# Attention sums normalised on GpSimd instead of on TensorE and VectorE, in a two-layer convolution kernel

## The chip, the cores and the metric

One core of one Trainium2 chip runs the kernel. The metric is the device time of one execution in microseconds (us). Engines by their names in the profile: PE is TensorE's matrix multiplication and PEld its weight load, DVE is VectorE, ACT is ScalarE, POOL is GpSimd, and SP (SPq) is the engine that issues the DMAs.

## The reference

The input is 16 images of 64 channels and 128 x 128 pixels, f32. Layer 0 adds a median term to every channel, upsamples by two with a 7-tap filter, applies a ReLU and downsamples again. Layer 1 gates the image in the frequency domain and runs an attention in which every pixel is a query and 320 positions (256 of a stride-8 and 64 of a stride-16 convolution) are keys, with 4 heads of 16 channels:

```python
attn = jax.nn.softmax(jnp.einsum('bhqd,bhkd->bhqk', q, k) * scale, axis=-1)
out = jnp.einsum('bhqk,bhkd->bhqd', attn, v)
out = out.transpose(0, 2, 1, 3).reshape(b, n, c)
out = out @ proj_w + proj_b
return out.transpose(0, 2, 1).reshape(b, c, h, w) + x
```

The change is in the last step of the softmax, the division of the weighted values by the sum of the weights, and in the projection behind it.

## The kernel before

The kernel loops over the 16 images. Each round has a convolution part, a spectrum part, the keys and values, and at its end the attention loop, which this change touches. Every engine has its own program (`tensor`, `vector`, `scalar`, `gpsimd`, `sync`) with the order of its work written out by hand; semaphores join them, and an engine that waits holds up all that is behind it in its own program.

The attention loop has NT = 32 tiles t of 512 queries. A tile has ten steps w. In step w TensorE computes one group of scores into PSUM bank 0 or 1 (`scores`, L735 for w below 8, L740 for 8 and 9) and ScalarE takes the exp (L1185); scores w wait for the exp of scores w - 2, because they share a bank. Beside this, in steps 0 to 7 of tile t, TensorE computes the maxima's matmuls of tile t + 2 (`maxima`, L714), which VectorE reduces (L978); at step 8 VectorE splits the reduced maxima in two bf16 parts (`split_max`, a cast at L986 and a subtraction at L988), TensorE transposes them at step 1 of the next tile (`lay_max`, L722), ScalarE copies them (L1168), and SP lays them into the queries by DMA (L1336).

The weighted values of tile t - 1 are summed on TensorE at steps 2, 4 and 7 of tile t (`weigh`, L760) into bank 7: 128 partitions of values and sums of weights by 512 queries. What follows is the part that the change replaces:

- ScalarE copies bank 7 to OR at step 8 (L1180).
- TensorE transposes it to queries by channels at step 9 (`denominators`, four transposes, L770).
- VectorE takes the reciprocal of the sums (L1010) and multiplies (L1014) at step 0 of the next tile.
- TensorE transposes back at step 4 (`turn_back`, two transposes, L778); ScalarE copies to OX (L1192).
- TensorE multiplies by the projection at step 6 (`project_out`, L785); VectorE adds the result to the image in SBUF (Z) at step 7 (L1024).

The loops run over t up to NT + 1 for that, so two tiles' rest comes behind the last scores, with a few filler matmuls (`busy`).

Some tiles carry more. `stage` computes the queries of later tiles at the steps named in STAGES: in tiles 0, 1, 4 to 7 and 12 to 15, a matmul on TensorE (L649, in bank 7 behind the reader of the sums), an activation on ScalarE (L1145), a subtraction on VectorE (L931), a cast and a subtraction on GpSimd (L1268, L1270). SP loads the next units of queries (`load_unit`, six DMAs a tile, L394), in tiles 24 to 27 the next image (`load_image`, two DMAs a tile), and at tile 28 half of the one after (`load_next`). GpSimd adds the median to the next image (`add_median`, L384, two additions of 128x1024 in each of the tiles 28 to 31 of its program, which runs ahead of the others as soon as the loads have landed). In the depthwise convolution of the values, ahead of the loop, GpSimd multiplies (L1283) and adds (L1287).

## Time and profile before

| | |
|---|---|
| median of 3 runs | 11580.47 us (11576.59 to 11598.01) |
| profiled execution, its own time | 11584.36 us |
| its span | 11582.8 us |
| busy: TensorE, VectorE, ScalarE, GpSimd | 90%, 76%, 63%, 24% |
| granted TensorE clock, mean | 0.978 |

All rows are from that one execution. Its span runs from the first to the last instruction; the own time is 1.6 us longer. The last image's attention loop lies at the span's end, so its times are near 11250 to 11570. "x" is a count; a row of a timeline gives the start, the length and what was done; an arrow with an engine behind it names what ended a wait.

### The profile page before, as it was taken

To read this page: it belongs to the slowest core of one execution; us is meant where nothing else is said; L and a number is where in the kernel's file an instruction comes from. 1 tells how busy PE (TensorE), PEld (TensorE's weight loads), DVE (VectorE), ACT (ScalarE), POOL (GpSimd) and SP (SyncE) were. 2 spreads that over 40 slices of the span, in tenths; PEclk is the share of its full clock that TensorE was granted. 3 is DMA by queue.
4 is the path that set the end of the run, shared out by engine and by line. 5 is a ranking of instruction groups with operands and counts; after the bars stand their busy time and mean duration, and the time that the engine had idled before them with its cause. 6 is when DMAs were issued, how large, how long until landed. Compare 5 with 4: busy or idle time off the path is not lost. (4 is left out here: it accounts for less than half of the span.)

```text
span 11582.8 us, 198561 instructions
## 1 busy us (share of the span) xinstructions
PE 10455.8 (90%) x71885; PEld 5275.3 (46%) x72029; DVE 8796.4 (76%) x15082; ACT 7250.1 (63%) x12109; POOL 2763.8 (24%) x5217
## 2 busy tenths in 40 slices
PE   2898998989989899899989989899898998989999
PEld 1544445344454544535445354444534445354453
DVE  7877777777777777778777787777777777777776
ACT  5667565675656757567575666756567565675756
POOL 2313213122131221312223131221312213122130
PEclk9999999999999999999999999999999999999999
DMA  2021221212213022130211302122121221202213
GB/s 65 20 47 46 47 64 29 49 35 51 60 31 59 31 48 56 35 61 34 42 51 42 69 20 47 46 47 64 30 52 32 52 59 32 57 31 50 54 37 74
DMA packets 176857, 537.70 MB, mean 46 GB/s; under 512 B 64904, under 2 KB 87560, under 8 KB 154448
## 3 DMA queue, kind: packets, MB, share of 16 engines
q1 hardware_dynamic: 175952, 525.31, 20.1%
q8 instruction: 608, 9.96, 0.4%
q14 instruction: 297, 2.43, 0.1%
HBM read 232.49 MB, written 71.30 MB: 26 GB/s over the span
## 5 line engine op out<-in xcount | busy, mean ns | idle before, releaser
L978 DVE TENSOR_REDUCE R<-ps 128x2 f32<-128x640 f32 x4096 | 3185.4, 818 | 906.3 <-PE ps L714 904.8
L1185 ACT ACTIVATE R<-ps 128x512 f32<-128x512 f32 x5120 | 2821.4, 594 | 654.5 <-PE ps L735 628.9
L258 ACT ACTIVATE R<-R,st 128x1475 bf16<-128x1475 f32 (+1 forms) x1326 | 2077.1, 1566 | 489.6 <-DVE st L330 464.9
L319 DVE TENSOR_SCALAR_CACHE_REDUCE R<-R,st 128x1255 bf16<-128x1255 f32 (+1 forms) x1326 | 1936.8, 1461 | 18.5
L714 PE MATMUL ps<-KST,R 96*128 96x320 bf16 x8192 | 1811.8, 302 | 38.8 <-DVE R L978 29.5
L760 PE MATMUL ps<-R 128*32 128x512 f32 x12288 | 1641.0, 607 | 37.9 <-DVE Wk L931 32.8
L735 PE MATMUL ps<-R,KST 104*128 104x512 bf16 x4096 | 1569.6, 386 | 36.9 <-ACT R L1185 23.7
L714 PEld LDWEIGHTS ps<-KST,R 96*128 96x128 bf16 x8192 | 757.6, 99 | 736.6 <-DVE R L978 223.8
L1268 POOL CAST R<-Wk 128x512 bf16<-128x512 f32 x256 | 283.8, 1109 | 2492.7 <-DVE Wk L931 2492.7
L735 PEld LDWEIGHTS ps<-R,KST 104*128 104x128 bf16 x4096 | 395.7, 97 | 724.3 <-ACT R L1185 461.3
L384 POOL TENSOR_TENSOR R<-R,sB 128x1024 f32<-128x1024 f32 x132 | 251.3, 1924 | 1641.4 <-DMA R<-xh_in 1635.9
L1145 ACT ACTIVATE R<-ps,cst 128x512 bf16<-128x512 f32 x256 | 176.0, 688 | 694.2 <-PE ps L649 694.2
L487 PE MATMUL ps<-R,cst 64*128 64x512 f32 x2048 | 549.7, 610 | 63.4 <-ACT R L1079 54.5
L498 PE MATMUL ps<-R,cst 128*64 128x512 f32 x2048 | 552.9, 618 | 18.0 <-ACT R L1079 18.0
L1192 ACT ACTIVATE Wk<-ps 128x256 f32<-128x256 f32 x512 | 196.6, 384 | 555.3 <-PE ps L778 555.3
L1072 ACT ACTIVATE R<-ps 128x532 f32<-128x532 f32 x512 | 312.8, 611 | 363.0 <-PE ps L477 354.3
L1180 ACT ACTIVATE Wk<-ps 128x512 f32<-128x512 f32 x512 | 305.7, 597 | 368.5 <-PE ps L760 368.5
L1079 ACT ACTIVATE R<-ps 128x1024 f32<-128x1024 f32 x512 | 517.7, 1011 | 16.7 <-PE ps L487 16.7
L416 PE MATMUL ps<-cst,identb 128*128 128x512 bf16 x1632 | 478.9, 386 | 51.8 <-issue 20.2
L215 PE MATMUL ps<-st,cst 128*128 128x10 f32 (+1 forms) x884 | 170.4, 266 | 380.0 <-ACT R L258 149.8
L1168 ACT ACTIVATE Wk<-ps 8x512 bf16<-8x512 bf16 x512 | 298.1, 582 | 292.9 <-PE ps L722 292.9
L760 PEld LDWEIGHTS ps<-R 128*32 128x32 f32 x12288 | 247.9, 108 | 458.1 <-issue 366.8
(211 smaller groups left out, 19167.0 us busy)
## 6 DMA issues: line engine op xcount, KB each, us to landing
R<-R SPq DMA_DIRECT2D x3072, 64.0 KB, 2.4
R<-xh_in SPq DMA_DIRECT2D x136, 512.0 KB, 4.4
out_dram<-Z SPq DMA_DIRECT2D x68, 1024.0 KB, 3.9
R<-xa_in SPq DMA_DIRECT2D x36, 1024.0 KB, 10.0
R<-xb_in SPq DMA_DIRECT2D x36, 1024.0 KB, 12.0
R<-sr_in SPq DMA_DIRECT2D x32, 1024.0 KB, 5.1
R<-sr_in SPq DMA_DIRECT2D x16, 2016.0 KB, 9.2
R<-sr_in SPq DMA_DIRECT2D x16, 1056.0 KB
```

The lines of the kernel that those rows point to most:

```text
L258: e.activation(junka[:, 0:o2 - o1], xc[:, o1:o2], ACT.Sign, bias=mid, scale=-1.0, accum_out=ca[i]).then_inc(md_ca, 1)
L319: e.tensor_scalar(junk[:, 0:o1 - o0], xc[:, o0:o1], mid, None, ALU.is_le, ALU.add, accum_out=cv[i]).then_inc(md_cv, 1)
L416: e.matmul(ps[:, bank, :], lhsT=identb[:, :], rhs=cst[:, 0:256].bitcast(BF16), start=True, stop=True)
L487: op = e.matmul(ps[:, 2 + j, :].rearrange("p (c h n) -> p c h n", c=2, h=2), lhsT=ut[r, 133 * j:133 * j + 128], rhs=T1[m % 2][r].rearrange ...
L498: op = e.matmul(ps[64 * j:64 * j + 64, 4, :], lhsT=c(f"d{j}"), rhs=Y[m % 2][:, j, :], start=True, stop=True)
L714: op = e.matmul(ps[:, 2 + 2 * bq + r, 0:320], lhsT=q, rhs=KST[0:96, h0 + r, :], start=True, stop=True)
L735: op = e.matmul(ps[:, g2, :], lhsT=KST[:, h, c0:c0 + 128], rhs=QS[u % 3][:, h, 512 * s4:512 * s4 + 512], start=True, stop=True)
L760: op = e.matmul(ps[32 * h:32 * h + 32, 7, :], lhsT=VX[:, 4 * i + h, :], rhs=PB[:, k, src, :], start=i == 0, stop=i == 2)
L978: e.tensor_reduce(MX[(4 * u + s4) % 2][:, blk_, h0:h0 + 2], ps[:, 2 + 2 * bq:4 + 2 * bq, 0:320], axis=AX.X, op=ALU.max).then_inc(mx, 1)
L1072: e.activation(T1[n % 2].rearrange("p h c n -> p h (c n)"), ps[:, 0:2, 0:266], ACT.Copy).then_inc(t1, 1)
L1079: e.activation(Y[m % 2], ps[:, 2:4, :], ACT.Relu, scale=4.0).then_inc(yr, 1)
L1185: e.activation(PB[:, t % 2, w, :], ps[:, w % 2, :], ACT.Exp).then_inc(ex, 1)
```

## The change

The division leaves TensorE and VectorE for all but the last two tiles. VectorE copies bank 7 to OR (`sums`, at step 8, ahead of `split_max`). The columns of values and sums of weights are interleaved (the strides of `values` are changed for this), so that every second partition of OR holds the sum that belongs to the partition before it. SP lays OR out by four DMAs a tile (`lay_out`): the values to XO and the sums to XD, 128 partitions by 256 queries, the first half of the queries on partitions 0 to 63 and the second on 64 to 127, two buffers each. GpSimd's `normalise(t - 2)` in tile t computes the reciprocal of XD (an integer estimate and three Newton steps) and multiplies XO by it, eleven instructions of 128x256, each waiting for the one before; it begins when the projection of the tile before has read XN2. TensorE's `project_out(t - 3)` stands at step 5 of tile t and reads XN2; VectorE's addition to Z is at step 7 as before. ScalarE's two copies are gone from the loop. `add_median` is spread, one addition in each of the tiles 24 to 31, behind `normalise`. The last two tiles are still turned on TensorE, behind the last scores.

```diff
--- before.py
+++ after.py
...
+NEAR = float(0x7EF311C7)
...
-ON = W[:, 1024:1280]
-OX = W[:, 1280:1536]
+XO = [W[:, 1024 + 256 * i:1280 + 256 * i] for i in range(2)]
+XD = [R2[:, 1024 + 256 * i:1280 + 256 * i] for i in range(2)]
+XI, XN2, ON, OX = (R2[:, 1536 + 256 * i:1792 + 256 * i] for i in range(4))
...
+def lay_out(e, t):
+    src = OR[t % 2]
+    row = src.ap[0][0]
+    e.wait_ge(ou, t + 1)
+    if t > 1:
+        e.wait_ge(on, t - 1)
+    for k, dst in enumerate((XD[t % 2], XO[t % 2])):
+        for half in range(2):
+            e.dma_start(dst[64 * half:64 * half + 64, :],
+                        bass.AP(src.tensor, src.offset + (1 - k) * row + 256 * half, [[2 * row, 64], [1, 256]])
+                        ).then_inc(in_o[t % 2], 16)
+
...
             op.then_inc(pv_ps, 1)
             b7[0] = (ou, t + 1)
-    def denominators(t):
-        e.wait_ge(ou, t + 1)
-        e.wait_ge(*b6[0])
-        for i in range(4):
-            op = e.transpose(ps[:, 6, 128 * i:128 * i + 128], OR[t % 2][:, 128 * i:128 * i + 128], c("ident"))
-        op.then_inc(den_ps, 1)
-        b6[0] = (on, t + 1)
-
-    def turn_back(t):
+    def project_out(t):
         e.wait_ge(on, t + 1)
         e.wait_ge(*b6[0])
         for i in range(2):
-            op = e.transpose(ps[:, 6, 128 * i:128 * i + 128], ON[:, 128 * i:128 * i + 128], c("ident"))
+            op = e.matmul(ps[:, 6, 128 * i:128 * i + 128], lhsT=XN2[:, 128 * i:128 * i + 128], rhs=c("pw"),
+                          start=True, stop=True)
+        op.then_inc(po_ps, 1)
+        b6[0] = (zo, t + 1)
+
+    def turn(t):
+        e.wait_ge(ou, t + 1)
+        for i in range(4):
+            op = e.transpose(ps[:, 2 + t % 2, 128 * i:128 * i + 128], OR[t % 2][:, 128 * i:128 * i + 128], c("ident"))
+        op.then_inc(den_ps, 1)
+
+    def turn_back(t):
+        e.wait_ge(od, t - NT + 3)
+        for i in range(2):
+            op = e.transpose(ps[:, 4 + t % 2, 128 * i:128 * i + 128], ON[:, 128 * i:128 * i + 128], c("ident"))
         op.then_inc(ot_ps, 1)
-        b6[0] = (ox, t + 1)
-
-    def project_out(t):
-        e.wait_ge(ox, t + 1)
+
+    def project_back(t):
+        e.wait_ge(ox, t - NT + 3)
+        e.wait_ge(*b6[0])
         for i in range(2):
             op = e.matmul(ps[:, 6, 128 * i:128 * i + 128], lhsT=OX[:, 128 * i:128 * i + 128], rhs=c("pw"),
                           start=True, stop=True)
...
             maxima(0, t, i)
             busy(0, 2)
         lay_max(t)
-    for t in range(NT + 2):
+    for t in range(NT):
         u, s4, ahead = t // 4, t % 4, t + AHEAD
-        live, prev, done2 = t < NT, 0 <= t - 1 < NT, t >= 2
         for w in range(10):
-            if live:
-                scores(t, w)
+            scores(t, w)
             if t == 0 and w == 8:
                 values()
-            if w < 8 and live and ahead < NT:
+            if w < 8 and ahead < NT:
                 maxima(ahead // 4, ahead % 4, w)
             if w == 1 and t and t + AHEAD - 1 < NT:
                 lay_max(t + AHEAD - 1)
-            if w in WEIGHS and prev:
+            if w in WEIGHS and t:
                 weigh(t - 1, WEIGHS.index(w))
-            if w in (4, 6) and t == NT + 1:
-                busy(0, w // 2)
-            if w == 4 and done2:
-                turn_back(t - 2)
-            if w == 6 and done2:
-                project_out(t - 2)
-            if w == 9 and prev:
-                denominators(t - 1)
+            if w == 5 and t > 2:
+                project_out(t - 3)
             if (t, w) in STAGES:
                 stage(*STAGES[t, w])
+    e.wait_ge(mx, 8 * NT)
+    turn(NT - 2)
+    weigh(NT - 1, 0)
+    weigh(NT - 1, 1)
+    project_out(NT - 3)
+    turn_back(NT - 2)
+    weigh(NT - 1, 2)
+    project_back(NT - 2)
+    busy(0, 2)
+    turn(NT - 1)
+    busy(0, 2)
+    turn_back(NT - 1)
+    busy(0, 2)
+    project_back(NT - 1)
     busy(0, 5)
...
-    def denominators(t):
-        heads = ps[:, 6, :].rearrange("p (a d) -> p a d", a=16)
-        e.wait_ge(den_ps, t + 1)
-        e.reciprocal(RD[t % 2], heads[:, :, 16]).then_inc(rc, 1)
-        if t:
-            e.wait_ge(ot_ps, t)
-        e.wait_ge(rc, t + 1)
-        e.tensor_tensor(ON.rearrange("p (a d) -> p a d", a=16), heads[:, :, 0:16],
-                        RD[t % 2].unsqueeze(2).to_broadcast([128, 16, 16]), ALU.mult).then_inc(on, 1)
-
-    def project_out(t):
+    def sums(t):
+        e.wait_ge(pv_ps, t + 1)
+        if t > 1:
+            e.wait_ge(in_o[t % 2], 64 * (t // 2))
+        e.tensor_copy(OR[t % 2], ps[:, 7, :]).then_inc(ou, 1)
+
+    def rest(t, order):
         u, s4 = t // 4, t % 4
         w0 = 2 * (16 * (u // 2) + 4 * s4) + u % 2
         zo_ = Z[:, :, w0:w0 + 7:2]
         e.wait_ge(po_ps, t + 1)
         if t == 0:
             e.wait_ge(zb, 4)
-        e.tensor_tensor(zo_, ps[:, 6, 0:256].rearrange("p (w c) -> p c w", w=4), zo_, ALU.add).then_inc(zo, 1)
+        if order:
+            zo_ = zo_.rearrange("p c (b i) -> p c b i", b=2)
+            po = ps[:, 6, 0:256].rearrange("p (i b c) -> p c b i", i=2, b=2)
+        else:
+            po = ps[:, 6, 0:256].rearrange("p (w c) -> p c w", w=4)
+        e.tensor_tensor(zo_, po, zo_, ALU.add).then_inc(zo, 1)
+
+    def divide(t):
+        heads = ps[:, 2 + t % 2, :].rearrange("p (a d s) -> p a d s", a=16, s=2)
+        n = t - NT + 3
+        e.wait_ge(den_ps, n)
+        e.reciprocal(RD[t % 2], heads[:, :, 0, 1]).then_inc(rc, 1)
+        if n > 1:
+            e.wait_ge(ot_ps, n - 1)
+        e.wait_ge(rc, n)
+        e.tensor_tensor(ON.rearrange("p (a d) -> p a d", a=16), heads[:, :, :, 0],
+                        RD[t % 2].unsqueeze(2).to_broadcast([128, 16, 16]), ALU.mult).then_inc(od, 1)
     for t in range(AHEAD):
         for i in range(8):
             maxima(0, t, i)
         split_max(t)
-    for t in range(NT + 2):
+    for t in range(NT):
         u, s4, ahead = t // 4, t % 4, t + AHEAD
-        live, prev, done2 = t < NT, 0 <= t - 1 < NT, t >= 2
         for w in range(10):
-            if w == 0 and done2:
-                denominators(t - 2)
-            if w == 7 and done2:
-                project_out(t - 2)
-            if w < 8 and live and ahead < NT:
+            if w == 7 and t > 2:
+                rest(t - 3, True)
+            if w < 8 and ahead < NT:
                 maxima(ahead // 4, ahead % 4, w)
-            if w == 8 and live and ahead < NT:
+            if w == 8 and t:
+                sums(t - 1)
+            if w == 8 and ahead < NT:
                 split_max(ahead)
             if t == NT - 1 and w in (1, 4):
                 e.wait_ge(in_xc[0], 32)
...
+    divide(NT - 2)
+    rest(NT - 3, True)
+    sums(NT - 1)
+    rest(NT - 2, False)
+    divide(NT - 1)
+    rest(NT - 1, False)
...
-    for t in range(NT + 2):
+    for t in range(NT):
         u, s4 = t // 4, t % 4
-        live, prev = t < NT, 0 <= t - 1 < NT
         for w in range(10):
-            if w == 8 and prev:
-                e.wait_ge(pv_ps, t)
-                if t > 2:
-                    e.wait_ge(den_ps, t - 2)
-                e.activation(OR[(t - 1) % 2], ps[:, 7, :], ACT.Copy).then_inc(ou, 1)
-            if live:
-                e.wait_ge(sc_ps, 10 * t + w + 1)
-                if w == 0 and t > 1:
-                    e.wait_ge(pv_ps, t - 1)
-                e.activation(PB[:, t % 2, w, :], ps[:, w % 2, :], ACT.Exp).then_inc(ex, 1)
+            e.wait_ge(sc_ps, 10 * t + w + 1)
+            if w == 0 and t > 1:
+                e.wait_ge(pv_ps, t - 1)
+            e.activation(PB[:, t % 2, w, :], ps[:, w % 2, :], ACT.Exp).then_inc(ex, 1)
             if w == 1 and t and t + AHEAD - 1 < NT:
                 lay_max(t + AHEAD - 1)
-            if w == 4 and t >= 2:
-                e.wait_ge(ot_ps, t - 1)
-                if t > 2:
-                    e.wait_ge(po_ps, t - 2)
-                e.activation(OX, ps[:, 6, 0:256], ACT.Copy).then_inc(ox, 1)
             if (t, w) in STAGES:
                 stage(*STAGES[t, w])
+    for n in range(2):
+        e.wait_ge(ot_ps, n + 1)
+        if n:
+            e.wait_ge(po_ps, NT - 2 + n)
+        e.activation(OX, ps[:, 4 + n, 0:256], ACT.Copy).then_inc(ox, 1)
...
+    def normalise(t):
+        k, n = t % 2, 10 * t
+        e.wait_ge(in_o[k], 64 * (t // 2 + 1))
+        if t:
+            e.wait_ge(po_ps, t)
+        e.tensor_scalar(XI.bitcast(I32), XD[k].bitcast(I32), -1.0, NEAR, ALU.mult, ALU.add).then_inc(nt, 1)
+        for _ in range(3):
+            e.wait_ge(nt, n + 1)
+            e.tensor_tensor(XN2, XD[k], XI, ALU.mult).then_inc(nt, 1)
+            e.wait_ge(nt, n + 2)
+            e.tensor_scalar(XN2, XN2, -1.0, 2.0, ALU.mult, ALU.add).then_inc(nt, 1)
+            e.wait_ge(nt, n + 3)
+            e.tensor_tensor(XI, XN2, XI, ALU.mult).then_inc(nt, 1)
+            n += 3
+        e.wait_ge(nt, n + 1)
+        e.tensor_tensor(XN2, XO[k], XI, ALU.mult).then_inc(on, 1)
+
...
-    for t in range(NT + 2):
-        u, s4 = t // 4, t % 4
-        live, prev = t < NT, 0 <= t - 1 < NT
+    for t in range(NT):
         for w in range(10):
             if (t, w) in STAGES:
                 stage(*STAGES[t, w])
-            if w == 9 and live and u == 7:
-                for k in (2 * s4, 2 * s4 + 1):
-                    e.wait_ge(in_xh[k], 16)
-                    add_median(e, k)
+            if w == 4 and t > 1:
+                normalise(t - 2)
+            if w == 9 and t >= NT - 8:
+                k = t - NT + 8
+                e.wait_ge(in_xh[k], 16)
+                add_median(e, k)
...
         for v, t0 in LOADS.items():
             if t0 <= t < t0 + 4:
                 load_unit(e, v, 6 * (t - t0), 6 * (t - t0) + 6)
+        if 0 < t < NT - 1:
+            lay_out(e, t - 1)
```

## Rows read from the trace of the kernel before

**Rows 1.** The page's part 1: busy time, share of the span and instructions of each engine.
```profile
PE 10455.8 (90%) x71885; PEld 5275.3 (46%) x72029; DVE 8796.4 (76%) x15082; ACT 7250.1 (63%) x12109; POOL 2763.8 (24%) x5217
```

**Rows 2.** Windows of the last loop: length; busy PE, PEld, DVE, ACT, POOL; clock; DMA.
```profile
11254.50:11275.10 20.60, 20.04 (x136) 8.35 (x136) 16.14 (x28) 13.98 (x27) 2.71 (x3) 1.00 0.26 43
11284.90:11328.20 43.30, 41.73 (x274) 17.64 (x274) 32.64 (x57) 28.85 (x56) 7.08 (x8) 1.00 0.35 56
...
11410.70:11479.30 68.60, 67.44 (x464) 27.89 (x464) 51.92 (x92) 47.43 (x92) 0.00 (x0) 1.00 0.28 45
11479.30:11542.90 63.60, 59.66 (x398) 24.20 (x396) 49.98 (x79) 40.76 (x79) 15.00 (x8) 0.97 0.38 103
11542.90:11559.30 16.40, 15.41 (x98) 4.99 (x96) 7.09 (x11) 13.04 (x26) 0.00 (x0) 1.00 0.02 3
11559.30:11569.80 10.50, 8.23 (x56) 3.61 (x54) 2.22 (x6) 2.90 (x6) 0.00 (x0) 1.00 0.87 186
```

**Rows 3.** Timeline of a plain tile: start, us, engine, line, operation, count, [idle before <-releaser].
```profile
11417.09 0.44 PE L778 MATMUL ps<-cst,Wk 128*128 128x128 f32 x2
...
11417.36 0.38 PE L735 MATMUL ps<-R,KST 104*128 104x512 bf16 x1
...
11418.35 0.61 PE L785 MATMUL ps<-cst,Wk 128*128 128x128 f32 x4
...
11418.79 0.38 PE L735 MATMUL ps<-R,KST 104*128 104x512 bf16 x1
...
11419.21 0.60 ACT L1185 ACTIVATE R<-ps 128x512 f32<-128x512 f32 x1 [0.28 <-PE ps L735]
...
11420.37 0.62 PE L740 MATMUL ps<-R,KST 104*64 104x512 bf16 x4
...
11421.16 0.66 PE L770 MATMUL ps<-cst,Wk 128*128 128x128 f32 x4 [0.17 <-ACT Wk L1180]
...
11421.74 0.38 PE L735 MATMUL ps<-R,KST 104*128 104x512 bf16 x1
```

**Rows 4.** Groups by line and shape, whole span, VectorE: busy us, mean ns, idle before.
```profile
L849 DVE COPY R<-ps 128x512 f32<-128x512 f32 x512 | 351.8, 687 | 92.6 <-PE ps L498 92.2
```

**Rows 5.** Timeline of GpSimd and VectorE around the end of a tile, without and with GpSimd busy.
```profile
11479.68 0.18 DVE L988 TENSOR_TENSOR R<-R 128x16 bf16<-128x16 f32 x1
...
11487.64 3.75 POOL L384 TENSOR_TENSOR R<-R,sB 128x1024 f32<-128x1024 f32 x2 [81.66 <-DMA R<-xh_in]
...
11489.26 0.32 DVE L986 CAST R<-R 128x16 bf16<-128x16 f32 x1
11489.61 1.82 DVE L988 TENSOR_TENSOR R<-R 128x16 bf16<-128x16 f32 x1
```

**Rows 6.** Groups on GpSimd, whole span (L1268: its line's durations, min/median/max ns).
```profile
L1270 POOL TENSOR_TENSOR R<-Wk,R 128x512 bf16<-128x512 f32 x256 | 301.9, 1179 | 20.5
...
L1283 POOL TENSOR_SCALAR R<-R,cst 64x256 f32<-64x256 f32 x144 | 135.7, 943 | 228.0 <-ACT R L1157 217.0
...
L278 POOL TENSOR_SCALAR st<-st 128x1 f32<-128x1 f32 x442 | 100.4, 227 | 1458.8 <-DVE st L326 1445.4
...
L1287 POOL TENSOR_TENSOR R<-R 64x256 f32<-64x256 f32 x128 | 92.2, 720 | 10.7
...
L1283 POOL TENSOR_SCALAR R<-R,cst 64x64 f32<-64x64 f32 x144 | 62.9, 439 | 11.0
...
L1268 POOL CAST R<-Wk x256: 609/611/2605, 545.5 to 11404.1; 128x512 bf16<-128x512 f32 x128
```

**Rows 7.** Timeline of GpSimd in the depthwise convolution of the values.
```profile
11210.29 0.72 POOL L1287 TENSOR_TENSOR R<-R 64x256 f32<-64x256 f32 x1
11211.10 0.92 POOL L1283 TENSOR_SCALAR R<-R,cst 64x256 f32<-64x256 f32 x1
```

**Rows 8.** An issue of six loads on SP's queue (timeline), and the DMA view's row for them.
```profile
11406.01 3.69 SPq L394 DMA_DIRECT2D R<-R  x6
...
R<-R SPq DMA_DIRECT2D x3072, 64.0 KB, 2.4
```

More of the change, by code:

```diff
@@ L9 @@
 BF16 = mybir.dt.bfloat16
+I32 = mybir.dt.int32
 ALU = mybir.AluOpType
@@ L161, in program @@
         zst = [zst0, zst1, zst2, zst3]
-        in_xc, in_w2, in_qs, in_m = [in_xc0, in_xc1], [in_w20, in_w21, in_w22], [in_qs0, in_qs1, in_qs2], [in_m0, in_m1]
+        in_xc, in_w2, in_qs, in_m, in_o = [in_xc0, in_xc1], [in_w20, in_w21, in_w22], [in_qs0, in_qs1, in_qs2], [in_m0, in_m1], [in_o0, in_o1]
         ut = c("ut")
```

16 lines of the change are left out of this document (8 added, 8 removed), and 4 rows, old and new, of the table SIGNALS.

## Prediction

> **What bounds the kernel now.** I read four views, in this order. The page says that TensorE is busy for 90% of the span, VectorE for 76%, ScalarE for 63% and GpSimd for 24% [rows 1]: TensorE leads, but this is a mean over stages. The windows over the last image's attention loop say what holds there. Seven tiles without other work take 68.6 us, 9.80 us a tile, and TensorE is busy in 67.44 of them; four tiles that also carry a query stage take 43.3 us, 10.83 a tile; TensorE's granted clock is 1.00, its upper level (2.4 GHz), and GpSimd does nothing in the plain tiles [rows 2]. From tile 1's last scores (11254.5) to the image's end (11569.8) it is 315.3 us, the first and the last edge of these windows. The diff touches this part of each of the 16 images, and little else: `values` writes the same number of instructions with other strides, once per image, which I count as nothing.
>
> The timeline of one plain tile shows where TensorE's time goes at the two places that the change empties [rows 3]. `turn_back` (L778) starts at 11417.09 and the next scores at 11417.36: 0.27 us. At the tile's end the last two scores (L740) start at 11420.37, the four transposes (L770) wait for ScalarE's copy, start at 11421.16, and the next tile's first scores start at 11421.74: 1.37 us.
>
> **TensorE's part.** Both transposes leave the loop. The 0.27 us goes whole. Of the 1.37 us not all goes, because a new wait stands behind it: scores 0 of the next tile need the bank that the exp of scores 8 frees. An exp starts 0.42 us after its scores start (11418.79 to 11419.21) and takes 0.60 [rows 3], so that exp ends 1.02 after 11420.37, and with a hand-over of 0.05 the scores start at about 11421.44: 0.30 us saved. So a plain tile could fall from 9.80 to 9.23 us, no lower. In a stage tile the query matmul needs bank 7, which VectorE's copy, behind its last reduction and 0.1 longer, frees some 0.35 us later than ScalarE's did (an estimate), so of the transposes' 0.55 about 0.2 is saved, 0.47 us with `turn_back`. ScalarE loses two copies and is not on the path afterwards.
>
> **VectorE's part.** It loses a reciprocal and a multiply and gains the copy of the sums, 0.69 us by the nearest row, the same shape from PSUM to SBUF [rows 4]; the totals are about equal. But the copy stands ahead of `split_max`, whose result `lay_max` on TensorE needs in the next tile. Unhindered that is in time, by some 0.7 us.
>
> It will be hindered. While GpSimd ran two 1.87 us additions (L384), `split_max`'s cast took 0.32 us, and its subtraction, 0.18 us when free, took 1.82: it waited for a whole GpSimd instruction [rows 5]. The cast slips in at the boundary between two GpSimd instructions, the subtraction then waits for the next one. Today GpSimd is idle in a plain tile, so this costs nothing; after the change it computes nearly all the time. The price lies between nothing (both fall into an idle stretch) and two instructions of about 0.75, 1.5 us; I take half an instruction and one whole, 1.0 us less the 0.7 of slack: 0.3 us of TensorE's wait. So TensorE and VectorE alone would make a plain tile of about 9.5 us, between 9.2 and 10.0.
>
> **GpSimd's part** decides. `normalise` is eleven dependent instructions of 128x256 f32 per tile, seven with two tensors and four with one tensor and two constants.
> - Two tensors: the 64x256 f32 addition of L1287 takes 0.72 us [rows 6]. Seven are 5.04.
> - One tensor: the only rows are L1283, 0.92 us for 64x256 in rows of 16 and 0.44 for 64x64 in rows of 8, both with a scalar per partition, and L278, 0.23 for one element with constants [rows 6]. If the step from one element to 64 holds a fixed price of the scalar, the slope is (0.92 - 0.44)/192 = 2.5 ns an element, and 256 cost 0.23 + 0.64 = 0.87. If it holds a price per row of the pattern instead, the slope is 2.07 ns and 256 cost 0.76. The lower bound is a cast, one input and no arithmetic: 0.61 for twice the elements [rows 6], so about 0.42 for 256. The upper one is 0.92 and a little, should the second operation cost something. I take 0.82, between the two readings of the same operation: four are 3.28.
> - Between dependent instructions there are 0.09 us (11211.01 to 11211.10) [rows 7]: ten are 0.90. `split_max` holds GpSimd up in its turn, by its own 0.2 us or so a tile; that stays inside the margin of the 0.82.
>
> Together 9.22 us. The Trainium skill, "GPSIMD Engine Reference", section "Engine selection", says that GpSimd is about twice as slow as VectorE on two inputs but roughly at line rate on one; the cast agrees with the second half and L1283 does not. By that rule `normalise` would be near the cast's end of the bounds, about 7.6 us, and the time the first rival's; by L1283 it is the forecast's.
>
> `normalise(t)` also waits for `project_out(t - 1)`, because XI and XN2 have one buffer, and `project_out(t - 1)` waits for `normalise(t - 1)`. So a round is `normalise`, 0.05 to TensorE, `project_out` (0.61, L785 [rows 3]) and 0.09 back: 9.97 us. That is above TensorE's 9.5 and above today's 9.80. In eight rounds a query stage stands behind `normalise` on GpSimd, 0.61 + 0.09 + 1.18 = 1.88 [rows 6], of which the return of 0.75 hides under it: 1.13 more. In seven an `add_median` of 1.87 [rows 5] stands there: 1.12 more.
>
> **DMA and SP.** Four transfers of 64 KB a tile are new on SP's queue. An issue takes 0.6 us (six in 3.69) and a 64 KB transfer lands after 2.4 us [rows 8], so a tile's sums are laid out 4.8 us after the copy. `normalise` wants them only a tile later: nothing. SP now waits for VectorE at each tile's end, and the next `lay_max` DMA is queued behind the four issues, 0.6 x 4 = 2.4 us; its data come only at step 1 of the next tile, and its reader is a further tile away: nothing. If the 1 MB loads of tile 28 hold one layout up, it is hidden while GpSimd runs late, else up to some 3 us once per image.
>
> **The sum.** From tile 1's last scores to the first `project_out` (tile 3): a stage tile of 10.36, a plain one of about 9.3 and 2.5 back, 17.2 us. Then 29 rounds to `project_out(29)`: 29 x 9.97 + 8 x 1.13 + 7 x 1.12 = 306.0. Behind it still come the third part of the last `weigh` and the last tile's whole turn, about 6.2 of the 10.5 us that now follow the last scores [rows 2]. Together 329.4 against 315.3: 14.1 us more in each image, 226 in 16. The profiled execution took 11584.4 us, 1.6 more than its span and 3.9 more than the median shown, 11580.5. So 11580.5 + 226 = 11806, say 11800. A hundredth of a us on the scalar instruction moves this by 0.01 x 4 x 29 x 16 = 18.6 us.
>
> **The rivals.**
> - *GpSimd keeps up, and the kernel is faster.* If the four scalar instructions run near the cast's rate, 0.4 to 0.6 us, a round is 8.3 to 9.1 us and TensorE sets the pace. For it: the cast's row. Against it: L1283, the same operation at 0.92. It decides below about 0.68 us. Up to 11479.3 thirteen plain tiles save 0.3 each and nine stage tiles 0.47, together 8.1. The six tiles from 11479.3 now take 63.6, partly because of the blocked subtraction [rows 2, 5]; with one addition each they take about 9.9, 4.2 less. The last two tiles and what follows (16.4 + 10.5 [rows 2]) get about 7 longer, since the last `normalise` is still running when the scores end. That is 5.3 us an image and 85 in all: 11495. Chance 0.28.
> - *The two meet.* The scalar instruction takes 0.66 to 0.70, or the blocked `split_max` costs TensorE 0.6 instead of 0.3, so that the plain tiles gain nothing, and what stage tiles save the longer end takes: 11580 within 0.2%. Chance 0.10.
> - *The second operation costs more.* The scalar instruction takes 0.92 as the row has it, or more, with two operations in place of one: 11800 + 10 x 18.6 = 11990. For it: the row is the only one of its size. Against it: its pattern and its scalar are costlier than constants on a plain tile. Chance 0.17.
>
> **How the numbers follow.** My forecast has 0.45 and covers scalar instructions of 0.72 to 0.90, 11610 to 11950. Slower adds the third rival: 0.62. The range must reach both the first rival, 11495, and the third, 11990, with a bit beyond either; 11470 to 12010 leaves out the scalar instruction near its lower bound and one well above 0.92. 0.2% is 23 us, 1.4 us an image, about what a measurement of this kernel can tell from no change.
>
> **What would show it.** The profile after should show four scalar instructions per tile near 0.8 us on GpSimd, GpSimd busy for over 85% of the loop, and TensorE's longest wait in the loop at `project_out`, released by GpSimd, with tiles of about 10 us, and about 11 where a stage or an addition stands on GpSimd. `split_max`'s two instructions should be longer than 0.18 us in most tiles. I am wrong if TensorE's wait there is short and the tiles come at 9.3 to 9.6: then the scalar instruction was mis-sized. If the tiles lie near 10 with GpSimd idle in between, the wait at `lay_max` or the new DMAs took its place.

## The result and the profile after

The kernel after takes 11460.19 us (median of 4 runs, 11451.31 to 11464.64) against 11580.85 us (median of 4 runs of the kernel before): a ratio of 0.9891, 95% interval 0.9876 to 0.9906, so 1.1% faster. The forecast was 11800 us, slower; the result lies just below the range, on the side of the first rival (11495). The profiled span is 11450.0 us against 11582.8.

The page's busy line, which answers to [rows 1]:

```profile
PE 10082.2 (88%) x69021; PEld 4987.8 (44%) x69165; DVE 8883.2 (78%) x14634; ACT 6859.4 (60%) x11117; POOL 5977.4 (52%) x10497
```

GpSimd's busy time has more than doubled, as foreseen, but it does not lead: inside the loop it is 47 of 65 us. That is the fifth row of the windows that answer to [rows 2]: the last image from tile 1's last scores to tile 23's, then to tile 29's, to tile 31's and to the image's end; then seven plain tiles and three stage tiles by themselves.

```profile
11129.73:11345.26 215.53, 201.03 (x1338) 76.91 (x1334) 177.80 (x273) 136.07 (x251) 159.43 (x253) 1.00 0.38 75
11345.26:11400.97 55.71, 52.30 (x364) 20.07 (x360) 46.47 (x73) 36.04 (x66) 48.13 (x68) 1.00 0.53 146
11400.97:11420.26 19.29, 14.95 (x89) 3.83 (x86) 7.50 (x9) 11.40 (x21) 17.34 (x25) 0.91 0.10 30
11420.26:11436.95 16.69, 11.76 (x64) 5.87 (x62) 4.03 (x9) 1.85 (x4) 8.34 (x12) 0.80 0.58 126
11289.61:11354.55 64.94, 60.97 (x426) 23.50 (x422) 54.92 (x85) 42.05 (x77) 47.11 (x77) 1.00 0.39 86
11248.70:11280.34 31.64, 29.34 (x191) 11.30 (x187) 25.50 (x40) 19.34 (x36) 25.33 (x39) 1.00 0.29 61
```

A plain tile takes 64.94 / 7 = 9.28 us (9.80 before), a stage tile 10.55 (10.83). Stage by stage the last image's ledger is:

| last image, us | before [rows 2] | after | difference | first rival's term |
|---|---|---|---|---|
| tile 1's last scores to tile 23's | 224.8 | 215.5 | -9.3 | -8.1 |
| tiles 24 to 29 | 63.6 | 55.7 | -7.9 | -4.2 |
| tiles 30, 31 | 16.4 | 19.3 | +2.9 | } +7 |
| last scores to the image's end | 10.5 | 16.7 | +6.2 | } |
| sum | 315.3 | 307.2 | -8.1 | -5.3 |

Sixteen times 8.1 is 130 us, the spans differ by 132.8. (The 224.8 are 315.3 less the other three.) In the last two stretches the granted clock is 0.91 and 0.80 in the mean, below the upper level (2.4 GHz) of the tiles before: TensorE waited 2.25, 0.72 and 3.86 us for the last three `normalise`, and the clock fell to the lower level (1.2 GHz) behind the first of these waits and during the third. That is part of the longer end. The other images divide their gain a little differently: in the mean of all 16 the loop from tile 1's last scores to tile 31's takes 291.3 us in place of 303.6, and from the last scores to the next image's first matmul it is 17.1 in place of 13.4.

The groups of `normalise` on GpSimd hold what went wrong with the forecast; L1337 is the line that was L1283 in [rows 6].

```profile
L1317 POOL TENSOR_TENSOR R<-R 128x256 f32<-128x256 f32 x1440 | 1050.1, 729 | 115.4
L1321 POOL TENSOR_TENSOR R<-R 128x256 f32<-128x256 f32 x1440 | 1045.4, 726 | 120.0
L1319 POOL TENSOR_SCALAR R<-R 128x256 f32<-128x256 f32 x1440 | 591.3, 411 | 126.3
L1324 POOL TENSOR_TENSOR R<-Wk,R 128x256 f32<-128x256 f32 x480 | 349.4, 728 | 37.6
...
L1314 POOL TENSOR_SCALAR R<-R 128x256 int32<-128x256 int32 x480 | 194.1, 404 | 598.0 <-PE ps L785 575.0 <-DMA Wk<-Wk 15.2
...
L1337 POOL TENSOR_SCALAR R<-R,cst 64x256 f32<-64x256 f32 x144 | 135.5, 942 | 227.7 <-ACT R L1201 216.7
```

The two-tensor instructions take 0.726 to 0.729 us (0.72 predicted). The scalar ones take 0.404 and 0.411, half of the 0.82 that was put in, while L1337 still takes 0.94 for fewer partitions. GpSimd, before L1314, waited 575.0 us in all for the projection: it is early, not late.

The timeline of a tile's end, the place of [rows 3 and 5], shows the two waits that the prediction set against each other.

```profile
11289.61 0.62 PE L755 MATMUL ps<-R,KST 104*64 104x512 bf16 x4
...
11290.04 0.68 DVE L1038 COPY Wk<-ps 128x512 f32<-128x512 f32 x1
...
11290.47 0.73 POOL L1317 TENSOR_TENSOR R<-R 128x256 f32<-128x256 f32 x1
11290.64 0.60 DVE L1013 CAST R<-R 128x16 bf16<-128x16 f32 x1
...
11290.81 0.38 PE L750 MATMUL ps<-R,KST 104*128 104x512 bf16 x1 [0.57 <-ACT R L1222]
...
11291.27 0.18 DVE L1015 TENSOR_TENSOR R<-R 128x16 bf16<-128x16 f32 x1
11291.29 0.43 POOL L1319 TENSOR_SCALAR R<-R 128x256 f32<-128x256 f32 x1
```

From the last scores to the next tile's first it is 1.20 us (1.37 before, 1.07 predicted), 0.57 of it the foreseen wait for the exp. The exp starts 0.45 behind its scores and takes 0.60, and the next scores start 0.15 behind its end, where the prediction had 0.05. `split_max`'s cast (L1013) is held up while L1317 runs, 0.60 in place of 0.18 (the medians of all 512 are 0.594 and, before, 0.179); but its subtraction (L1015) slips in before GpSimd's next, dependent instruction and takes 0.18. The Trainium skill, "SBUF — State Buffer", section "Who interferes with whom", says that a VectorE instruction in a mode that takes both of its port pairs, which a cast can be in, and GpSimd keep each other out of the pair that they share: whoever issues first has it for the whole instruction. The cast agrees (0.60); the subtraction shows that the gap of 0.085 us between GpSimd's dependent instructions is enough for VectorE to be first.

### The profile page after: what moved, and what is told of

The parts are those of the page before. It is cut to its first block and busy times, and to the rows that moved or that the text cites. A ratio compares the mean times of both kernels' runs of the same rounds, so it can differ in the third digit from the quotient of the medians.

```text
span 11450.0 us, 198049 instructions
## 1 busy us (share of the span) xinstructions
PE 10082.2 (88%) x69021; PEld 4987.8 (44%) x69165; DVE 8883.2 (78%) x14634; ACT 6859.4 (60%) x11117; POOL 5977.4 (52%) x10497
## 5 line engine op out<-in xcount | busy, mean ns | idle before, releaser
L1005 DVE TENSOR_REDUCE R<-ps 128x2 f32<-128x640 f32 x4096 | 3225.6, 819 | 920.0 <-PE ps L729 860.3
L1317 POOL TENSOR_TENSOR R<-R 128x256 f32<-128x256 f32 x1440 | 1050.1, 729 | 115.4
L1321 POOL TENSOR_TENSOR R<-R 128x256 f32<-128x256 f32 x1440 | 1045.4, 726 | 120.0
L281 POOL TENSOR_SCALAR st<-st 128x1 f32<-128x1 f32 x442 | 99.4, 225 | 1459.7 <-DVE st L329 1446.3
L1275 POOL TENSOR_TENSOR R<-R 128x24 f32<-128x24 f32 x512 | 119.9, 234 | 1258.8 <-DVE R L890 1258.8
L1319 POOL TENSOR_SCALAR R<-R 128x256 f32<-128x256 f32 x1440 | 591.3, 411 | 126.3
L1314 POOL TENSOR_SCALAR R<-R 128x256 int32<-128x256 int32 x480 | 194.1, 404 | 598.0 <-PE ps L785 575.0
```

The lines of the kernel that those rows point to most:

```text
L1005: e.tensor_reduce(MX[(4 * u + s4) % 2][:, blk_, h0:h0 + 2], ps[:, 2 + 2 * bq:4 + 2 * bq, 0:320], axis=AX.X, op=ALU.max).then_inc(mx, 1)
L1317: e.tensor_tensor(XN2, XD[k], XI, ALU.mult).then_inc(nt, 1)
L1319: e.tensor_scalar(XN2, XN2, -1.0, 2.0, ALU.mult, ALU.add).then_inc(nt, 1)
L1321: e.tensor_tensor(XI, XN2, XI, ALU.mult).then_inc(nt, 1)
```

## The experiments

**1. Which part of L1283 costs 0.92.** Nine multiplies of the depthwise convolution, five of them in other forms:

```diff
+if t9 == 1:
+    op = e.tensor_scalar(part, rows, 0.5, None, ALU.mult)
+elif t9 == 2:
+    op = e.tensor_scalar(part, flat, sc, None, ALU.mult)
+elif t9 == 3:
+    op = e.tensor_scalar(part, flat, 0.5, None, ALU.mult)
+elif t9 == 4:
+    op = e.tensor_scalar(part, flat, -0.5, 2.0, ALU.mult, ALU.add)
+elif t9 == 5:
+    op = e.tensor_scalar(part, rows, -0.5, 2.0, ALU.mult, ALU.add)
...
```

> The kernel after, with GpSimd's nine multiplies of the depthwise convolution (64x256 f32) in five forms on lines of their own: its own form (rows of 16 in a wider map, a scalar per partition), a constant with the same rows, a scalar per partition with a plain tile, a constant with a plain tile, and two constants with each pattern; most taps of that convolution are so left out. Theory: my bound of 0.92 us was the price of the pattern of rows and not of the operation, so a plain tile takes about 0.41 us with a constant and with a scalar per partition, and rows take about 0.9 in every form; a second constant costs under 0.03. Rival: it was the price of the scalar per partition, so both forms with one take about 0.9 and both with a constant about 0.41. If both halves count, each mixed form lies between, near 0.65. The whole time should stay at 11460 within 20 us.

The groups on GpSimd by form: L1349 is the unchanged line, L1339, L1341, L1343, L1345 and L1347 are the five of the diff in its order, the last two with two operations.

```profile
L1349 POOL TENSOR_SCALAR R<-R,cst 64x256 f32<-64x256 f32 x64 | 60.7, 948 | 221.8 <-ACT R L1201 216.9
...
L1339 POOL TENSOR_SCALAR R<-R 64x256 f32<-64x256 f32 x16 | 15.2, 950 | 0.0
L1341 POOL TENSOR_SCALAR R<-cst 64x256 f32<-64x256 f32 x16 | 14.7, 917 | 1.7
L1343 POOL TENSOR_SCALAR R<-cst 64x256 f32<-64x256 f32 x16 | 13.5, 842 | 1.4
...
L1347 POOL TENSOR_SCALAR R<-R 64x256 f32<-64x256 f32 x16 | 6.4, 400 | 1.4
L1345 POOL TENSOR_SCALAR R<-cst 64x256 f32<-64x256 f32 x16 | 6.4, 398 | 1.4
```

Theory and rival both fall. With one operation every form takes 0.84 to 0.95: the scalar per partition costs 0.075, the rows 0.03 to 0.11. With two operations, rows or not, it takes 0.40. The second operation, which I feared might cost something, halves the price. The whole time, 11446 us in one run, moved by 14, too little for one run to tell.

**2. The price put back, by the form.** The kernel after with the additions of the four scalar instructions left out:

```diff
-e.tensor_scalar(XI.bitcast(I32), XD[k].bitcast(I32), -1.0, NEAR, ALU.mult, ALU.add).then_inc(nt, 1)
+e.tensor_scalar(XI.bitcast(I32), XD[k].bitcast(I32), -1.0, None, ALU.mult).then_inc(nt, 1)
...
-e.tensor_scalar(XN2, XN2, -1.0, 2.0, ALU.mult, ALU.add).then_inc(nt, 1)
+e.tensor_scalar(XN2, XN2, -1.0, None, ALU.mult).then_inc(nt, 1)
```

> The kernel after, with the second operation of normalise's four scalar instructions left out (times -1 alone, no constant added; the reciprocal is so not computed). By the run with the depthwise forms, one operation with a constant takes 0.84 us on a plain 64x256 tile and two take 0.40. Theory: it was the form that I priced, so with one operation these instructions cost what the row of before has, 0.84: normalise 7.56 + 4 x 0.43 = 9.3 us, a round 9.3 + 0.93 = 10.2, and the time, between the runs with two and with four scalar instructions more (8.54 us: 11603, 9.50 us: 12054), is about 11960: doing less, the kernel is 500 us slower. That is my forecast's case. Rival: the price belongs to the depthwise operands (64 partitions, other places) and not to the form: 0.40, and no change, 11460.

Measured: 11932.8 us (one run). Two groups, and a window over six plain tiles (10.28 us each):

```profile
L1319 POOL TENSOR_SCALAR R<-R 128x256 f32<-128x256 f32 x1440 | 1223.5, 850 | 126.2
...
L1314 POOL TENSOR_SCALAR R<-R 128x256 int32<-128x256 int32 x480 | 408.5, 851 | 235.8 <-PE ps L785 235.8
```

```profile
11763.10:11824.80 61.70, 53.83 (x365) 20.01 (x361) 47.32 (x73) 36.06 (x66) 51.14 (x66) 1.00 0.35 79
```

With less arithmetic the kernel is 473 us slower, and it is the forecast's case: at 0.85 the prediction's rule (18.6 us per hundredth) gives 11806 + 56 = 11862, and with the return below, 0.18 us a round longer than the 0.75 put in, 29 x 16 x 0.18 = 84 more, 11946.

**3. The price put back, by number.** Each scalar instruction is followed by one that changes nothing; all four in the first run, two of them in the second:

```diff
+e.tensor_scalar(XI, XI, 1.0, 0.0, ALU.mult, ALU.add).then_inc(nt, 1)
...
+e.tensor_scalar(XN2, XN2, 1.0, 0.0, ALU.mult, ALU.add).then_inc(nt, 1)
```

> The kernel after, with each of the four scalar instructions of normalise followed by a second one that changes nothing (times 1, plus 0), so that the four cost about what my forecast took them to cost: 4 x (0.41 + 0.085) = 1.98 us more, normalise 9.5 us. Theory (only the price was wrong, the round was right): GpSimd decides, a plain tile is normalise and a return of 0.75, about 10.3 us, and the time by the prediction's own sum with 10.29 in place of 9.97 is 17.2 + 29 x 10.29 + 8 x 1.13 + 7 x 1.12 + 6.2 = 338.7 against 315.3 us an image: 11955. Rival: the return is hidden and normalise alone makes the tile, 9.5 us: about 11600. Second rival: GpSimd isn't on the path, and only the image's end grows by 2 us: 11490.

> The kernel after, with two of the three scalar instructions in the Newton steps followed by a second one that changes nothing: normalise 7.56 + 2 x 0.49 = 8.54 us. It lies between the kernel after and the run with four of them, where a round was normalise and 0.93. Theory: GpSimd decides from a normalise of 9.28 - 0.93 = 8.35 us on, so this one is just above: plain tiles of 8.54 + 0.93 = 9.47 in place of 9.28, stage tiles still 10.55, the tiles with an addition 0.98 longer, the end 1 us longer: 15 x 0.19 + 7 x 0.98 + 1 = 10.7 us an image, 11630. Rival: GpSimd's idle time of 1.7 us a tile in the kernel after is all slack, so plain tiles stay at 9.28 and only the additions and the end cost: 7.9 us an image, 11585.

Measured: 12053.6 us with four and 11602.93 with two (one run each). A round's end with four, and windows over three plain tiles with four and seven with two:

```profile
11896.87 0.72 POOL L1331 TENSOR_TENSOR R<-Wk,R 128x256 f32<-128x256 f32 x1
...
11897.65 0.71 PE L785 MATMUL ps<-cst,R 128*128 128x128 f32 x4 [0.89 <-POOL R L1331]
...
11898.52 0.40 POOL L1314 TENSOR_SCALAR R<-R 128x256 int32<-128x256 int32 x1 [0.93 <-PE ps L785]
```

```profile
11910.69:11941.99 31.30, 26.92 (x184) 10.04 (x180) 23.46 (x37) 18.01 (x33) 25.03 (x45) 1.00 0.36 89
```

```profile
11432.72:11499.07 66.35, 62.37 (x424) 23.41 (x421) 52.61 (x85) 42.05 (x77) 52.87 (x91) 1.00 0.38 85
```

The return is 0.93 us and not 0.75 (the projection takes 0.71 when TensorE has waited). With four, a plain tile takes 10.43, and less the 0.93 that leaves 9.50 for `normalise`; with two, 8.54 + 0.93 = 9.47 and 9.48 measured. The whole time with four lies 99 us above the theory (11955), 84 of them for the longer return; with two it lies between the theory (11630) and the rival (11585), but the tiles are the theory's. The round decides as the prediction had it, from a `normalise` of 9.28 - 0.93 = 8.35 us on. The kernel after has 7.57 (first start 11287.87; the last starts at 11294.71 and takes 0.73).

**4. GpSimd's work taken away.** The three Newton steps of the kernel after are left out:

```diff
-for _ in range(3):
-    ...
 e.wait_ge(nt, n + 1)
 e.tensor_tensor(XN2, XO[k], XI, ALU.mult).then_inc(on, 1)
```

> The kernel after, without the three Newton steps of normalise: the first guess of the reciprocal alone is multiplied with the sums, so GpSimd does two instructions a tile (about 1.2 us) and its sums are only roughly normalised. Theory: TensorE, with the wait for the exp at each tile's edge, makes the plain tile of 9.28 us, and GpSimd costs it nothing there; the plain tiles stay at 9.2 to 9.3, the tiles with an addition fall from about 9.47 to 9.28, and the image's end gets shorter by 5 to 6 us, since no normalise is waited for: about 11370. Rival: GpSimd's running holds VectorE's split_max up and with it TensorE, by the 0.3 us that I predicted; then plain tiles fall to about 9.0 as well and the time to about 11260.

Measured: 11411.45 us (one run). Seven plain tiles:

```profile
11256.51:11321.44 64.93, 60.95 (x425) 23.49 (x422) 51.92 (x85) 42.03 (x77) 8.48 (x15) 1.00 0.39 86
```

GpSimd's busy time in them falls from 47.11 to 8.48 us and the tiles stay at 64.93 us. Neither GpSimd nor the held-up `split_max` (whose cast is back at 0.17) costs TensorE anything in a plain tile of the kernel after; the 0.3 us of the prediction was nothing. The time fell by 49, not by 90: the end got shorter, but the next image began late and at a lower clock (experiment 6).

**5. One part alone: the spread additions.** The kernel before with one `add_median` per tile:

```diff
-if w == 9 and live and u == 7:
-    for k in (2 * s4, 2 * s4 + 1):
-        e.wait_ge(in_xh[k], 16)
-        add_median(e, k)
+if w == 9 and NT - 8 <= t < NT:
+    k = t - NT + 8
+    e.wait_ge(sc_ps, 10 * t + 6)
+    e.wait_ge(in_xh[k], 16)
+    add_median(e, k)
```

> The kernel before, with its eight additions of the median (1.87 us on GpSimd) run one per tile in tiles 24 to 31, each after the tile's sixth scores, as the kernel after has them, and no other edit. Theory: the six tiles from 24 took 63.6 us because the pairs of additions held split_max up; spread, they come at about 9.9 us each, 59.2, so 4.4 us an image and 70 in 16: 11510. Then 4 to 5 of the 7.9 us that these six tiles gained between the two kernels are the spreading's, and the rest of the gain is that of the transposes. Rival: what those tiles lost lies in their loads and in the clock, and the spread changes nothing: 11580. Second rival: the spreading is the whole gain, 11460.

Measured: 11521.36 us, ratio 0.9954 (0.994 to 0.9967). Tiles 24 to 29:

```profile
11421.21:11479.98 58.77, 57.78 (x401) 23.84 (x398) 44.46 (x79) 40.62 (x78) 11.38 (x6) 1.00 0.41 112
```

The six tiles are plain ones now, 9.80 us each, 4.8 less than the 63.6 of [rows 2]. So 54 us (3.4 an image in the mean), nearly half of the whole gain of 121, come from a part of the change that has nothing to do with the division. The rest is the transposes' saving less the longer end.

**6. The end.** Three attempts to win back the longer end. First, three tiles in place of two turned on TensorE (tile 29's transposes stand in tile 31) and the last three additions behind the last `normalise`:

```diff
-if w == 4 and t > 1:
+if w == 4 and 1 < t < NT - 1:
     normalise(t - 2)
...
+if w == 1 and t == NT - 1:
+    e.wait_ge(mx, 8 * NT)
+    turn(NT - 3)
...
+for k in range(5, 8):
+    e.wait_ge(in_xh[k], 16)
+    add_median(e, k)
```

> The kernel after, with three tiles in place of two turned on TensorE (tile 29's transposes stand in tile 31, as before the change), so that no normalise runs on behind the last scores, and with the last three additions of the median behind the last normalise. Theory: the last two tiles and the end, 3 and 3 to 6 us longer than before the change, get most of that back: 5 to 7 us an image, 80 to 110 in all: 11365. Rival: the next image starts later on GpSimd, as it did where normalise was cut to two instructions (3.2 us from the barrier's end), and half of it is lost again: 11415.

Measured: 11463.48 us, ratio 0.9899 (0.9883 to 0.9916), no gain over the kernel after. The timelines from the next to last image's last scores to the start of the last image, the kernel after first:

```profile
10724.10 0.62 PE L755 MATMUL ps<-R,KST 104*64 104x512 bf16 x4
...
10737.42 0.43 DVE L1052 TENSOR_TENSOR Z<-ps,Z 128x256 f32<-128x256 f32 x1 [1.72 <-PE ps L806]
10739.85 0.38 POOL L1246 COPY R<-R 128x48 f32<-128x48 f32 x2 [8.19 <-POOLq L1516]
...
10740.39 0.60 PE L438 MATMUL ps<-cst,R 128*96 128x261 f32 x2
```

```profile
10733.18 0.62 PE L755 MATMUL ps<-R,KST 104*64 104x512 bf16 x4
...
10742.15 0.42 DVE L1059 TENSOR_TENSOR Z<-ps,Z 128x256 f32<-128x256 f32 x1 [1.72 <-PE ps L806]
...
10748.35 0.38 POOL L1261 COPY R<-R 128x48 f32<-128x48 f32 x2 [11.74 <-issue]
```

From the last scores to the end it is 13.75 us after (37.42 + 0.43 - 24.10) and 9.39 with three tiles; but GpSimd's first copy of the next image, which TensorE waits for, comes 2.0 us behind the end in the one and 5.8 in the other, so the next image starts 16.3 and 15.6 us after the last scores. In the mean of the 15 passages from image to image it is 17.1 and 15.3, and 13.4 before the change. So the end that was lengthened costs an image 3.7 us there, not the 6 of the last image, and a shorter one gives back 1.8.

That is lost again at once, to TensorE's clock. The stretch from an image's first matmul (L438) to its first transposes (L532) takes 9.37 us at all 15 starts of the kernel before and of the kernel after, at a granted clock of 1.00. With three tiles, where TensorE has little to do until that copy comes, it takes 11.5 to 14.3 us (12.7 in the mean) at 0.60 to 0.79. That it is the clock, and not the wait itself, shows in the second kernel of experiment 7, where GpSimd is late too: 9.45 us at the 13 starts with a clock of 1.00, 10.85 and 13.84 at the two with 0.84 and 0.63. The start shown above, the kernel after first:

```profile
10740.39:10749.76 9.37, 9.25 (x62) 4.20 (x61) 5.39 (x5) 5.75 (x8) 2.71 (x6) 1.00 0.18 73
```

```profile
10748.79:10761.00 12.21, 12.21 (x60) 5.76 (x61) 5.37 (x5) 5.78 (x8) 2.82 (x6) 0.72 0.13 53
```

From the last scores to those transposes it is 22.7 us before, 26.5 after and 28.0 with three tiles, in the mean.

Two further runs asked why GpSimd starts late: the last three additions on VectorE in tile 30, so that GpSimd is through before the load is issued; and the load issued behind the last sums.

```diff
+if w in (1, 3, 5) and t == NT - 2:
+    e.wait_ge(in_xh[5 + w // 2], 16)
+    add_median(e, 5 + w // 2)
```

```diff
 e.wait_ge(sc_ps, 320)
-load_next(e, it, 1)
 e.wait_ge(in_xc[0], 32)
 e.wait_ge(zo, NT)
+load_next(e, it, 1)
```

> Three tiles turned on TensorE as in the run before with them, but the last three additions of the median run on VectorE in tile 30, which has no maxima left, and not on GpSimd behind the last normalise. In that run the end was 4.4 us shorter than in the kernel after (9.4 against 13.75 from the last scores in the next to last image), and the next image began 3.7 us later, because GpSimd's first instruction came 14.5 us after the issue of the next image's 1 MB load in both runs that had this. Theory: GpSimd fetches the loop's first code when its own program is through, and where the load has been issued by then, the fetch waits for it; here GpSimd is through with normalise some 2.8 us before the load, so the image starts with the other engines again: 4 to 5 us an image, 64 to 80: 11385. Rival: the late start has another cause (a fixed price of a GpSimd that ends late): no change, 11460.

> Three tiles turned on TensorE and the last three additions behind the last normalise on GpSimd, as in the run before with both, with one edit: SP issues the next image's 1 MB load only when the image's last sums are written, 9 us later. Theory: GpSimd's fetch of the loop's first code is no longer behind that load, so GpSimd starts with the other engines and 3.5 us an image come back: 11460 - 56 = 11405, unless the load, now 9 us later, is wanted by the next image's first steps on VectorE before it has landed. Rival: the late start has nothing to do with the load: 11460. Second rival: the load is then late for VectorE by up to 9 us: 11460 to 11550.

Measured: 11511.51 us, ratio 0.994 (0.9926 to 0.9953), and 11541.25 us, 0.997 (0.9958 to 0.9982). Both theories fall as they stand. With GpSimd idle for 18.8 us it still started only 13.6 us after the issue. With the load issued later it started later too:

```profile
10799.84 1.19 SPq L380 DMA_DIRECT2D R<-xb_in  x2
...
10810.38 0.38 POOL L1261 COPY R<-R 128x48 f32<-128x48 f32 x2 [16.66 <-issue]
```

The load alone doesn't set GpSimd's start: in the kernel after it comes 2.0 us behind the image's end at all 15 passages, when the load has landed. (The load is two DMAs of 1 MB; the expectations count one.) Where the time goes in the run with three tiles its chain shows: behind the branch at the loop's end (L1526), which GpSimd alone is slow to leave. In that piece the DMA view has five transfers of the kind `instruction`.

```profile
10744.39 3.83 issue
10748.22 0.05 POOLq L1526
```

```profile
q14 instruction: 4, 0.03, 3.7%
q8 instruction: 1, 0.02, 2.9%
```

The records of all runs, 15 passages each, sort themselves:

| kernels | GpSimd's records in an image | the load lands | from GpSimd's branch to its next instruction | `instruction` transfers begun in between |
|---|---|---|---|---|
| before, experiment 5 | 427, 435 | 1.0 to 1.7 us behind the branch | 0.18 to 0.21 us | none |
| after, experiments 1 to 3, first kernel of 7 | 786 to 906 | 1.6 to 9.6 us ahead of it | 0.37 to 0.43 us | none |
| experiment 4, first two of 6, last two of 7 | 516 to 774 | 0.5 to 2.8 us behind it | 1.5 to 4.1 us | 4 or 5 |
| load issued behind the last sums | 774 | 10.5 to 11.2 us behind it | 6.8 to 10.0 us | 5 in 13 of 15 |

So GpSimd is late where its program is longer than before and the load is still on its way at the branch. The Trainium skill, "Runtime: NRT & Kernel Launch", section "Instruction fetch mechanics", says that a taken branch to code outside an engine's instruction window forces a DMA to fetch it; such a fetch, held up by the load, fits every row of the table. That the transfers are GpSimd's is not shown, as the view doesn't name the engine, and no run made GpSimd's program longer by itself.

The first of the two runs was slow for another reason, which its timeline shows:

```profile
10758.80 4.77 DVE L387 TENSOR_TENSOR R<-R,sB 128x1024 f32<-128x1024 f32 x3
...
10760.89 1.59 POOL L1335 TENSOR_TENSOR R<-R 128x256 f32<-128x256 f32 x1
```

VectorE's long additions more than double GpSimd's instructions (0.72 to 1.59), and `normalise` ends late: tile 30 takes 14.2 us, against 9.9 with the additions on GpSimd.

**7. The wait at the tile's edge.** `project_out` moved into the 0.57 us wait for the exp, and with it VectorE's addition to Z, which comes to stand behind `split_max`; then the same with three tiles turned on TensorE:

```diff
-if w == 5 and t > 2:
+if w == 9 and t > 2:
     project_out(t - 3)
...
-if w == 4 and t > 1:
+if w == 9 and t > 1:
     normalise(t - 2)
```

> The kernel after, with project_out moved from TensorE's step 5 behind the last scores of its tile, where TensorE waits 0.57 us for the exp of scores 8, VectorE's addition of the residue behind split_max, and normalise behind the tile's stage. Theory: that wait is the whole of what is left between TensorE's work and the tile of 9.28 us, and 0.6 us of project_out fit into it: plain tiles of 8.7, and in stage tiles the wait for the copy of the sums (0.55) is filled in the same way; 22 tiles x 0.5 = 11 us an image, less 2 to 4 for the end, where project_out comes later: 11460 - 16 x 8 = 11330. Rival: GpSimd's round, normalise 7.56 + 0.93 = 8.5, and lay_max, which now waits behind VectorE's addition of the residue in bank 6, hold plain tiles at 9.0 or more: 11400 to 11460.

> The two edits of the two runs before this one together (three tiles turned on TensorE, and project_out in the wait at the tile's edge). Theory: they add, since one works in the tiles and the other at the end: 11330 - 90 = 11240. Rival: the end is the bound that is common to both and only the larger one counts: 11330.

Measured: 11975.92 us, ratio 1.034 (1.0323 to 1.0357), and 11820.52, 1.0207 (1.019 to 1.0224). Plain tiles fell only to 9.21 us: the wait at the edge is filled (1.19 us from the last scores to the next ones, `project_out` in it), but the stretch that it left, from the maxima ahead of step 5 to the next `weigh`, went only from 1.79 to 1.73 us. In it TensorE's weight loads now wait, for an exp and for VectorE's reduction of the maxima (L1005):

```profile
11871.34 0.10 PEld L750 LDWEIGHTS ps<-R,KST 104*128 104x128 bf16 x1 [0.26 <-ACT R L1222]
...
11871.84 0.11 PEld L729 LDWEIGHTS ps<-KST,R 96*128 96x128 bf16 x2 [0.41 <-DVE R L1005]
```

And in both runs four tiles at each group of stages rose to between 12.0 and 15.8 us, by my own edit: GpSimd takes its work in order, and `normalise` now stood behind the stage, for whose data GpSimd waited.

```profile
11799.85 0.61 POOL L1305 CAST R<-Wk 128x512 bf16<-128x512 f32 x1 [5.15 <-DVE Wk L958]
...
11801.78 0.41 POOL L1314 TENSOR_SCALAR R<-R 128x256 int32<-128x256 int32 x1
```

So the order was turned round in the second of the two kernels:

```diff
+if w == 9 and 1 < t < NT - 1:
+    normalise(t - 2)
 if (t, w) in STAGES:
     stage(*STAGES[t, w])
-if w == 9 and 1 < t < NT - 1:
-    normalise(t - 2)
```

> The run with both edits (three tiles turned on TensorE, project_out in the wait at the tile's edge), with GpSimd's order in a stage tile changed: normalise stands ahead of the query stage and no longer behind it. In that run plain tiles were at 9.21 and the stage tiles ahead of the loop's stages at 10.32, but the stage tiles themselves took 13 to 15.7 us, because GpSimd waited 5.2 us for the stage's data with normalise queued behind. Theory: without that the eight stage tiles fall to about 10.4, 31 us an image and 500 in all: 11820 - 500 = 11320, which beats the kernel after. Rival: the stage, now behind normalise, comes a tile late, and the loads that wait for it (SP's queue, with lay_out behind them) hold tiles up: above 11460.

Measured: 11344.64 us, ratio 0.98 (0.9787 to 0.9813): 2.0% faster than the kernel before and 116 us below the kernel after. Seven plain tiles (9.21 each) and three stage tiles (10.32):

```profile
11188.82:11253.27 64.45, 63.66 (x424) 23.37 (x420) 52.53 (x85) 42.00 (x77) 47.04 (x77) 1.00 0.42 92
11148.65:11179.61 30.96, 29.94 (x192) 11.03 (x188) 24.51 (x40) 19.32 (x36) 25.31 (x40) 1.00 0.26 56
```

## Why the prediction was wrong

- **The step that failed** is the term "four scalar instructions at 0.82": they take 0.41. It was read from L1283, the only row of its size [rows 6], and both readings of that row (a price of the scalar, a price of the pattern) were of an instruction with one operation. (Its 0.92 is one instruction, of [rows 7]; the mean in [rows 6] is 0.943.) L1283 tells nothing of the form with two. L278, from which the price of one element came, has two operations, so the line through both joined two forms; and "should the second operation cost something" had the sign the wrong way. Four times 0.41 too much is 1.64 us, which alone carries `normalise` from 7.57 to 9.2, across the point of 8.35 from which it decides.
- **What followed from it was right.** Seven two-tensor instructions at 0.72, gaps of 0.09, and a round of `normalise` and a return hold to a few hundredths, but for the return (0.93, not 0.75). With the price put back a stage adds about 0.8 and an addition 0.9 us to a plain round (1.13 and 1.12 predicted), and the time is the forecast's within 1.1% (11932.8 against 11800). The nearness owes something to luck: the longer return and the cheaper rounds pull opposite ways. The kernel's 0.41 is the lower bound that was given, the cast's 0.42.
- **The rule that was weighed and set aside was the better guide.** The Trainium skill's "GPSIMD Engine Reference", section "4.1 Engine selection", has one-input work at roughly line rate; by it `normalise` was put near 7.6 us, and the trace has 7.57. The trace agrees for the form with two operations (0.41) and not for the one with one (0.85).
- **The blocked `split_max`** was priced at 0.3 us for TensorE and costs nothing: the cast is held up by 0.42, the subtraction is not, and the slack of 0.7 takes it. Which of the two is held up was the wrong way round: the subtraction had waited behind a GpSimd instruction that followed without a wait [rows 5], and in `normalise` each waits for the one before.
- **TensorE's floor** was right: 9.23 predicted, 9.28 found, with the wait for the exp where it was put. Its two parts were less close: the tile's edge gave 0.17 us and not 0.30, the rest of the tile 0.35 and not 0.27. In stage tiles 0.47 was predicted and 0.28 found.
- **The first rival's terms** were each too small: -8.1 for -9.3, -4.2 for -7.9, +7 for +9.1. Its 11495 is 35 us above the result, nearer than its terms deserve, as the errors partly cancel. The second term missed that the pairs of additions alone had cost 4.8 us and that tiles 24 to 29 gain as plain tiles besides, 0.5 each.
- **Copy, DMAs and SP** were right: the copy takes 0.68, a 64 KB layout lands after 2.0, and once in each image, in the last one behind the 2 MB load, a layout held `normalise` up, by 0.95 us (15.2 in 16).

## What to carry to other kernels

A price belongs to the exact form of an instruction: count its operations as well as its elements before a row is carried over, and where one term decides the sign and only a distant row prices it, give the other reading of it equal weight. What a change does on the side (here the spread of eight additions) may be half of its gain, so run it alone. And an in-order engine that is nearly full needs its queue's order chosen anew: the place of one call was worth 476 us here (11820.52 to 11344.64). A shorter end of a loop's round can be worth nothing, if the next round then starts with a wait behind which TensorE's clock is lower.

## What the runs showed of the hardware that was not expected

- On GpSimd a scalar instruction with one operation takes 0.84 to 0.95 us for 256 f32 a partition and with two operations 0.40, with 64 or 128 partitions, f32 or int32, plain or in rows.
- VectorE's short instruction can start in the 0.085 us between two dependent GpSimd instructions; a cast that comes while one runs waits for it (median 0.594 against 0.179 before), and long VectorE additions of two tensors stretch GpSimd's from 0.72 to 1.59.
- GpSimd took 0.18 us from the branch at the loop's end to its next instruction with 427 or 435 records in an image, a 2 MB load in flight. With 516 or more it took 0.37 where the load had landed, 1.5 to 4.1 where it landed up to 2.8 us behind the branch, and 6.8 to 10.0 where it had been issued 2.7 us before it.
- After such a late start TensorE was granted 0.60 to 0.79 of its clock for the image's first stretch in the run with three tiles, which took 11.5 to 14.3 us in place of 9.37.
